# A graph network's front phase: node products as half-row matmuls, taken in pairs

## The chip, the cores and the metric

One Trainium2 core runs the whole program. The metric is device time in microseconds (us), the median of three runs. Five engines work side by side: PE (TensorE; its weight loads are listed as PEld), DVE (VectorE), ACT (ScalarE), POOL (GpSimd) and SP (SyncE, which here only issues DMAs). They meet through semaphores.

## The reference, cut to what matters

Two layers of a graph network over 6250 nodes and 100000 edges. The front phase, which the change touches, computes the part of layer 0 that joins each edge with its node:

```python
s1 = jnp.einsum('ea,eb,abc->ec', xs, es, W1) * (1.0 / np.sqrt(MUL0_N * MUL0_E))
s2 = jnp.einsum('eai,ebi,abc->ec', xv, ev, W2) * (1.0 / (np.sqrt(3.0) * np.sqrt(MUL1_N * MUL1_E)))
out_s = (s1 + s2) * inv_sqrt2
v1 = jnp.einsum('ea,ebi,abc->eci', xs, ev, W3) * (1.0 / np.sqrt(MUL0_N * MUL1_E))
v2 = jnp.einsum('eai,eb,abc->eci', xv, es, W4) * (1.0 / np.sqrt(MUL1_N * MUL0_E))
out_v = (v1 + v2) * inv_sqrt2
...
agg = jax.ops.segment_sum(messages, row, num_segments=N_NODES)
```

Here `xs` are 64 scalars of a node and `xv` 32 vectors of three components; an edge has 8 scalars and 8 vectors (32 numbers).

## The kernel before

The kernel first multiplies nodes with the weights, not edges: for each block of 128 nodes a table `g` of 32 rows of 160 numbers a node is made (rows stand for the 32 edge numbers). The table goes to memory (`products`) and comes back, four nodes together, into a ring in SBUF (`quad_ring`). An edge's message is then a product of its own 32 numbers, placed by DVE into `front_work` where its node stands, with that ring.

**Tiles, pairs, chunks.** The 784 tiles have 128 edges each. Two tiles are a pair, two pairs a batch, eight pairs (k = 0 to 7) a chunk of 16 tiles; there are 49 chunks, and 49 blocks of nodes. The loops are unrolled in Python (`unrolled`), so each engine's order is the order in which the code calls the stages.

**PE, in one pair k of chunk i:** in every even pair `spread_ids` (L517, one product of one row, bf16) for a batch two ahead; `expand` (L544 and L549): seven f32 products of 160 columns, which the trace shows as 14 matmuls; in every odd pair `expand` begins with `load_words`, a register load of PE (L476); last `produce`: `unit(i + 3, k)` for k below 6, and `rank` (L506, L507) in pair 6.

**A unit** is one sixth of a block's table. Units 0 to 3 are a product of 128 rows with 512 columns (L492), units 4 and 5 two of 256 columns (L495, L496), all f32; the trace shows each product as two matmuls. The operands `x_alone` hold 64 or 32 rows of node features and zeros in all others, so that a full-height product picks the wanted part of the weights `w_first` (wa) and `w_second` (wb). The units fill two PSUM banks in turn; unit n waits for `units_taken` of n-2.

**ACT** copies in program order: `copy_pair` (L642, L644: messages out of PSUM, which frees one of three banks for `expand`), in odd pairs `spread_features` (L633, three copies) for the batch four ahead, in pairs 3 and 7 the load of a ring unit (L623), and then `take_unit` (L598, L601 to L605) for the same k. After unit 5 it stores the table (L609).

**DVE**, batch by batch: `build` (L836 to L849: with a register load of its own, L842; needs the batch's ids, its features, and that the batch three before has been expanded); after the build of a chunk's first batch `settle_places` (L815 to L826), which waits for the `rank` that PE does in pair 6 of the chunk before; after that of the second batch `tally` (L796 to L804). PE's `spread_ids` for batch n waits until the batches up to n-2 are built, `expand` of batch n until n is built.

**POOL** scatters each tile's messages (L451). **SP** loads ids, features and, once a chunk, the node features of a block (L398 to L401).

## Time and profile before

| | |
|---|---|
| median of 3 runs | 3041.04 us (3039.52 to 3052.91) |
| time of the profiled execution | 3042.78 us, of it 3041.0 us span |
| front phase: first to last matmul of L549 | 51 to 1325 us |
| PE busy in the span | 85% |
| granted TensorE clock, mean of the span | 0.928 |

A row of a timeline reads: start, duration, engine, line, operation, count, and in brackets how long the engine was idle before it and who ended that. Matmuls overlap: two L549 that begin at 848.39 and last 0.43 are two of 0.30 that begin 0.14 apart. So PE's time is read from start to start. The ends are modelled, and some waits are put down to "remote" or "issue" where no releaser is shown.

### The profile page before, as it was taken

How to read it: one execution, taken by the hardware profiler on the slowest of the kernel's cores; microseconds unless marked ns; L12 is line 12 of the kernel's file. 1: busy time of each engine (PE TensorE's matmuls, PEld its weight loads, DVE VectorE, ACT ScalarE, POOL GpSimd, SP SyncE). 2: the span in 40 equal slices, each digit the busy share in tenths (PEclk: the TensorE clock that was granted, in tenths of full speed). 3: DMA queues.
4: the chain of work that ended last, by engine and by line, in shares of the span. 5: the costliest groups of instructions: out<-in, count | busy, mean ns of one | idle time of the engine just before them, and what ended most of it. 6: DMA issues, size and time to landing. Idle time of an engine off the chain costs nothing. (4 is left out here: it accounts for less than half of the span.)

```text
span 3041.0 us, 51486 instructions
## 1 busy us (share of the span) xinstructions
PE 2570.8 (85%) x15408; PEld 2273.6 (75%) x15408; DVE 1878.6 (62%) x5408; ACT 1082.7 (36%) x2570; POOL 1584.4 (52%) x1677
## 2 busy tenths in 40 slices
PE   6989988989999999879999578787788777777787
PEld 4777777777777777769999478777777777777777
DVE  6666666666666676648878455555555555554555
ACT  4555555555555555512222122212222222121211
POOL 3656565565656656631010356655566556555553
PEclk9999999999999999989999698988988889888888
DMA  7888888888878888747888422222222222222221
GB/s 277 288 289 295 300 299 300 294 288 275 274 259 274 276 280 264 233 185 265 285 290 288 128 67 69 64 67 79 63 68 68 73 67 68 66 63 79 63 66 49
DMA packets 417284, 558.62 MB, mean 184 GB/s; under 512 B 73425, under 2 KB 354880, under 8 KB 404549
## 3 DMA queue, kind: packets, MB, share of 16 engines
q10 hardware_dynamic: 217680, 262.22, 25.7%
q1 hardware_dynamic: 120694, 153.35, 15.7%
q0 software_dynamic: 78640, 139.64, 15.4%
q8 instruction: 145, 2.38, 0.3%
q14 instruction: 125, 1.02, 0.1%
HBM read 326.92 MB, written 228.11 MB: 183 GB/s over the span
## 5 line engine op out<-in xcount | busy, mean ns | idle before, releaser
L1551 POOL DMA_INDIRECT f_y<-y_table,b_rec x782 | 767.9, 982 | 548.0 <-DVE f_msg L1634 310.3
L451 POOL DMA_INDIRECT placed<-message,slots_now x784 | 770.0, 982 | 536.0 <-ACT message L644 319.7
L544 PEld LDWEIGHTS g_bank<-quad_ring,front_work 128*128 128x128 f32 x4704 | 671.5, 193 | 187.4 <-issue 184.5
L544 PE MATMUL g_bank<-quad_ring,front_work 128*128 x4704 | 748.7, 309 | 72.7 <-issue 55.6
L1760 PE MATMUL e_bank<-f_msg,f_hot 128*126 128x160 f32 x1564 | 356.7, 333 | 212.8 <-DVE f_msg L1634 191.4
L846 DVE SCALAR_TENSOR_TENSOR front_work<-g_bank,quarter_node,front_work 128x512 f32<-128x512 f32 x588 | 404.7, 744 | 153.1 <-issue 101.3
L1760 PEld LDWEIGHTS e_bank<-f_msg,f_hot 128*126 128x126 f32 x1564 | 273.4, 209 | 240.0 <-DVE f_msg L1634 214.8
L1755 PE MATMUL e_bank<-f_msg,f_hot 128*126 128x160 f32 x1564 | 383.1, 329 | 25.3 <-DVE f_msg L1634 13.0
L1844 ACT COPY block_sums<-e_bank 126x320 f32<-126x320 f32 x196 | 83.4, 425 | 810.6 <-PE e_bank L1755 387.7
L633 ACT COPY front_work<-front_work 32x512 f32<-32x512 f32 x588 | 362.4, 616 | 13.2 <-issue 3.6
L1744 PE MATMUL e_bank<-fc,b_hidden 100*128 100x192 f32 x1564 | 342.4, 341 | 10.5 <-issue 10.5
L1620 DVE TENSOR_TENSOR e_bank<-e_bank,own 128x6 f32<-128x6 f32 x195 | 33.4, 171 | 499.8 <-remote 322.3
L644 ACT COPY message<-g_bank 128x320 f32<-128x320 f32 x392 | 168.3, 432 | 459.7 <-PE g_bank L549 269.4
L1755 PEld LDWEIGHTS e_bank<-f_msg,f_hot 128*126 128x126 f32 x1564 | 293.7, 212 | 30.4 <-issue 23.0
L1744 PEld LDWEIGHTS e_bank<-fc,b_hidden 100*128 100x128 f32 x1564 | 286.8, 203 | 22.5 <-issue 15.1
L1606 DVE SCALAR_TENSOR_TENSOR f_hot<-count_row,b_column,b_rec 128x168 f32<-128x168 f32 x782 | 270.9, 387 | 0.6 <-issue 0.6
L1219 PE MATMUL z_bank<-big,work 128*128 128x161 f32 x1764 | 254.7, 302 | 10.7 <-DVE work L1134 10.5
L1219 PEld LDWEIGHTS z_bank<-big,work 128*128 128x128 f32 x1764 | 245.5, 191 | 11.2 <-issue 10.7
L1634 DVE TENSOR_TENSOR f_msg<-e_bank,f_y 128x192 f32<-128x192 f32 x782 | 238.3, 345 | 0.0
L492 PE MATMUL g_bank<-w_first,x_alone 128*128 128x512 f32 x392 | 203.2, 603 | 14.7 <-DVE w_second L682 13.4
L1838 ACT ACTIVATE b_hidden<-e_bank 100x512 f32<-100x512 f32 x196 | 117.0, 597 | 225.3 <-PE e_bank L1735 101.1
L1631 DVE TENSOR_TENSOR f_msg<-e_bank,f_y 128x256 f32<-128x256 f32 x391 | 162.6, 416 | 54.7 <-issue 21.2
(252 smaller groups left out, 3199.4 us busy)
## 6 DMA issues: line engine op xcount, KB each, us to landing
products<-g ACTq DMA_DIRECT2D x49, 2560.0 KB
quad_ring<-products ACTq DMA_DIRECT2D x98, 1280.0 KB
big<-placed SPq DMA_DIRECT2D x48, 1458.0 KB, 7.1
b_lengths<-length_parts SPq DMA_DIRECT2D x294, 60.0 KB
placed<-zeros SPq DMA_DIRECT2D x24, 648.0 KB
front_work<-in_e_t SPq DMA_DIRECT2D x196, 64.0 KB
placed<-message,slots_now POOLq DMA_INDIRECT x784
f_y<-y_table,b_rec POOLq DMA_INDIRECT x782
```

The costliest lines, as they stand in the source:

```text
L451: pool.indirect_dma_start(v.placed[:, :], bass.IndirectOffsetOnAxis(slots_now[tile // SET % SLOT_SETS][:, tile % SET:tile % SET + 1], 0), ...
L492: last = pe.matmul(into[:], xs[j][:], wa[:], start=True, stop=True)
L544: pe.matmul(bank_now[:, n * D:n * D + D], spread[batch % SPREADS][:, j, q * P:q * P + P], ring[:, bass.ds(slot + j, 1), :].rearrange("p a ...
L633: last = act.copy(features[h][32 * n:32 * n + 32, :, :], features[h][0:32, :, :])
L846: dve.scalar_tensor_tensor(spread[batch % SPREADS][:, j, :], p_node[h % 2][:], v.quarter_node[:, j:j + 1], flat, ALU.is_equal, ALU.mult)
L1219: last = pe.matmul(p_agg[k % 2], hot[k % 2][:, j, :], placed_rows[k][:, j, 0:MW], start=(j == 0), stop=(j == ROWS - 1))
L1551: pool.indirect_dma_start(f_y[:, at, :], None, v.y_table[:, :], bass.IndirectOffsetOnAxis(b_rec[d % LOAD_RING][:, b % LOADED, 2 * c + n, 0 ...
L1606: dve.scalar_tensor_tensor(f_hot[:, r, :, :], v.count_row[:, 0:SUB].unsqueeze(1).broadcast_to([P, 4, SUB]), b_column[b % COLUMNS][:, j:j + 1],
L1634: last = dve.tensor_tensor(f_msg[:, r + n, :, S:D].rearrange("p g (i c) -> p g i c", i=3), w[:, n, 128:192].rearrange("p (g c) -> p g c", ...
L1744: last = pe.matmul(p_rad[pair % 3][:, 192 * n:192 * n + 192], b_hidden[b % HIDDEN_RING][:, 2 * c + n, :], v.fc2[:], start=True, stop=True)
L1755: return pe.matmul(p_acc[b % 2][0:3 * SUB, D:MSG], f_hot[:, r, 1:4, :].rearrange("p s n -> p (s n)"), f_msg[:, r, 1, :], start=(c == 0 and ...
L1760: return pe.matmul(p_acc[b % 2][0:3 * SUB, 0:D], f_hot[:, r, 0:3, :].rearrange("p s n -> p (s n)"), f_msg[:, r, 0, :], start=False, stop=F ...
```

## The change

The zero-padded operands go. A block's features come in two tiles, `x_parts`: the first has the 64 scalars in rows 0 to 63, vector component 0 in rows 64 to 95 and zeros to 127; the second has component 2 in rows 0 to 31, zeros to 95, component 1 in rows 96 to 127. Each product now uses the upper 64 or the lower 64 rows alone; a new weight tile `w_upper` (wc) has the vector weights in its first 32 rows and zeros below. The units alternate: 0, 2, 4 upper, 1, 3, 5 lower. Two units stand together behind pair 1, 3 and 5, and ACT takes two behind its pair 0, 2 and 4. The number of products and of columns is as before. SP issues two loads of features a block in place of four. At the start ACT issues two more weight loads, and DVE scales two more weight pieces and clears less.

```diff
-        wa, wb = sb("w_first", [P, 512]), sb("w_second", [P, 256])
-        alone = [[sb(f"x_alone{k}{m}", [P, P]) for m in range(4)] for k in range(2)]
+        wa, wb, wc = sb("w_first", [P, 512]), sb("w_second", [P, 256]), sb("w_upper", [S, 768])
+        parts = [[sb(f"x_parts{k}{m}", [P, P]) for m in range(2)] for k in range(2)]
...
+                act.dma_start(wc[0:V, 0:512], t["w2"]).then_inc(weights_in, 16)
+                act.dma_start(wc[0:V, 512:768], t["w4"]).then_inc(weights_in, 16)
...
-                    for m in range(4):
-                        dve.memset(alone[k][m][:], 0.0)
+                    dve.memset(parts[k][0][96:P, :], 0.0)
+                dve.memset(wc[V:S, :], 0.0)
...
-                    one, two, three, four = alone[b % 2]
-                    sp.dma_start(one[0:64, :], t["x_t"][0:64, at]).then_inc(x_in[b % 2], 16)
-                    sp.dma_start(two[64:96, :], t["x_t"][64:96, at]).then_inc(x_in[b % 2], 16)
-                    sp.dma_start(three[96:128, :], t["x_t"][96:128, at]).then_inc(x_in[b % 2], 16)
-                    sp.dma_start(four[64:96, :], t["x_t"][128:160, at]).then_inc(x_in[b % 2], 16)
+                    sp.dma_start(parts[b % 2][0][0:96, :], t["x_t"][0:96, at]).then_inc(x_in[b % 2], 16)
+                    sp.dma_start(parts[b % 2][1][:], t["x_rest_t"][:, at]).then_inc(x_in[b % 2], 16)
...
-                    if j < 4:
-                        last = pe.matmul(into[:], xs[j][:], wa[:], start=True, stop=True)
+                    upper, lower = slice(0, S), slice(S, P)
+                    if j == 0:
+                        last = pe.matmul(into[:], first[upper, :], wa[upper, :], start=True, stop=True)
+                    elif j == 1:
+                        last = pe.matmul(into[:], first[lower, :], wa[lower, :], start=True, stop=True)
+                    elif j == 2:
+                        last = pe.matmul(into[:], rest[upper, :], wc[:, 0:512], start=True, stop=True)
+                    elif j == 3:
+                        last = pe.matmul(into[:], rest[lower, :], wa[lower, :], start=True, stop=True)
+                    elif j == 4:
+                        pe.matmul(into[:, 0:256], first[upper, :], wb[upper, :], start=True, stop=True)
+                        last = pe.matmul(into[:, 256:512], rest[upper, :], wc[:, 512:768], start=True, stop=True)
                     else:
-                        m = 2 * (j - 4)
-                        pe.matmul(into[:, 0:256], xs[m][:], wb[:], start=True, stop=True)
-                        last = pe.matmul(into[:, 256:512], xs[m + 1][:], wb[:], start=True, stop=True)
+                        pe.matmul(into[:, 0:256], first[lower, :], wb[lower, :], start=True, stop=True)
+                        last = pe.matmul(into[:, 256:512], rest[lower, :], wb[lower, :], start=True, stop=True)
...
-                    if k < PARTS6:
+                    if k % 2 and k < PARTS6:
+                        unit(i + LEAD, k - 1)
                         unit(i + LEAD, k)
...
-                    if k < PARTS6:
+                    if k % 2 == 0 and k < PARTS6:
                         take_unit(i + LEAD, k)
+                        take_unit(i + LEAD, k + 1)
```

On PE, behind pair 4 of a chunk, stands before (L549 ends pair 4, L495 and L496 are unit 4, L476 the register load ahead of pair 5):

```order
L549 MATMUL g_bank<-quad_ring,front_work 128x160
L495 MATMUL g_bank<-w_second,x_alone 128x256
L496 MATMUL g_bank<-w_second,x_alone 128x256
L476 TENSOR_LOAD places
L544 REGISTER_ALU
L544 ISA
L544 MATMUL g_bank<-quad_ring,front_work 128x160
```

and now, where L553 and L558 are the lines of the same expansion and L475 that of the register load:

```order
L558 MATMUL g_bank<-quad_ring,front_work 128x160
L475 TENSOR_LOAD places
L553 REGISTER_ALU
L553 ISA
L553 MATMUL g_bank<-quad_ring,front_work 128x160
```

The register load of pair 5 follows pair 4 with no unit between them.

On PE, behind pair 5, stands before (L495, L496: unit 5; L517: the ids product ahead of pair 6):

```order
L549 ISA
L549 REGISTER_ALU
L549 MATMUL g_bank<-quad_ring,front_work 128x160
L495 MATMUL g_bank<-w_second,x_alone 128x256
L496 MATMUL g_bank<-w_second,x_alone 128x256
L517 MATMUL g_bank<-id_rows,ones 128x512
L544 REGISTER_ALU
```

and now:

```order
L558 ISA
L558 REGISTER_ALU
L558 MATMUL g_bank<-quad_ring,front_work 128x160
L501 MATMUL g_bank<-w_second,x_parts 128x256
L502 MATMUL g_bank<-w_upper,x_parts 128x256
L504 MATMUL g_bank<-w_second,x_parts 128x256
L505 MATMUL g_bank<-w_second,x_parts 128x256
L526 MATMUL g_bank<-id_rows,ones 128x512
L553 REGISTER_ALU
```

Units 4 (L501, L502) and 5 (L504, L505) now both stand there; units 0 and 1, 2 and 3 stand so behind pairs 1 and 3.

On ACT, from pair 2 to pair 4, stands before (L598 is the take of units 2 and 3):

```order
L644 COPY message<-g_bank 128x2x160
L598 COPY g<-g_bank 128x8x64
L644 COPY message<-g_bank 128x2x160
L633 COPY front_work<-front_work 32x512 x3
L623 DMA quad_ring<-products 128x16x160
L598 COPY g<-g_bank 128x8x64
L642 COPY message<-local 128x4
L644 COPY message<-g_bank 128x2x160
```

and now, where L609 is the take, L655 the message copy and L644 the copy of features:

```order
L655 COPY message<-g_bank 128x2x160
L609 COPY g<-g_bank 128x8x64 x2
L655 COPY message<-g_bank 128x2x160
L644 COPY front_work<-front_work 32x512 x3
L634 DMA quad_ring<-products 128x16x160
L653 COPY message<-local 128x4
L655 COPY message<-g_bank 128x2x160
```

The take of unit 3 has moved ahead of the message copy and the feature copies of pair 3.

## Rows read from the trace of the kernel before

**Rows 1.** Busy time by stretch; then PEclk, DMA share, GB/s. The last is without products.

```profile
800.00:1000.00 200.00, 183.19 (x1049) 145.78 (x1048) 133.96 (x294) 115.03 (x266) 119.69 (x124) 0.99 0.84 276
1277.00:1303.00 26.00, 22.14 (x120) 19.31 (x119) 14.47 (x30) 13.50 (x28) 16.00 (x17) 0.87 0.37 113
```

**Rows 2.** Line L549: count, duration min/median/max in ns, first and last start.

```profile
L549 PE MATMUL g_bank<-quad_ring,front_work x784: 296/299/474, 51.0 to 1324.7; 128*128 x196
```

**Rows 3.** Waits from 76 to 1250 us (45 chunks): total, times, longest.

```profile
DVE held L815 <- PE g_bank L507: 131.5, 31, 9.0
...
DVE held L815 <- remote: 65.3, 11, 7.7
...
DVE slots_now L836 <- ACT message L644: 31.0, 19, 2.6
...
PE g_bank L517 <- DVE front_work L849: 25.9, 31, 2.1
...
PEld g_bank L495 <- ACT g L598: 15.2, 18, 1.8
```

**Rows 4.** Timeline of PE, one chunk, from rank to rank.

```profile
830.69 0.39 PE L507 MATMUL g_bank<-held,ones 128*128 128x49 f32 x2
...
837.13 1.89 PE L544 MATMUL g_bank<-quad_ring,front_work 128*128 x12 [0.81 <-issue]
...
845.17 1.02 PE L492 MATMUL g_bank<-w_first,x_alone 128*128 128x512 f32 x2
846.12 0.38 PE L517 MATMUL g_bank<-id_rows,ones 1*128 1x512 bf16 x1
...
848.66 0.59 PE L495 MATMUL g_bank<-w_second,x_alone 128*128 128x256 f32 x2
...
851.43 0.43 PE L549 MATMUL g_bank<-quad_ring,front_work 128*128 x2
852.55 0.70 PE L495 MATMUL g_bank<-w_second,x_alone 128*128 128x256 f32 x2 [0.68 <-ACT g L598]
853.09 0.59 PE L496 MATMUL g_bank<-w_second,x_alone 128*128 128x256 f32 x2
853.61 0.39 PE L517 MATMUL g_bank<-id_rows,ones 1*128 1x512 bf16 x1
...
856.09 0.39 PE L507 MATMUL g_bank<-held,ones 128*128 128x49 f32 x2
```

**Rows 5.** Timeline of DVE in the same chunk.

```profile
831.11 0.21 DVE L815 TENSOR_TENSOR held<-held,r_count 128x49 f32<-128x49 f32 x1 [3.03 <-PE g_bank L507]
...
845.18 0.60 DVE L849 SCALAR_TENSOR_TENSOR front_work<-g_bank,quarter_node,front_work 128x128 f32 x2
```

**Rows 6.** Timeline of ACT in the same chunk, pair 3.

```profile
849.57 0.43 ACT L644 COPY message<-g_bank 128x320 f32<-128x320 f32 x1 [2.56 <-PE g_bank L549]
...
850.02 1.87 ACT L633 COPY front_work<-front_work 32x512 f32<-32x512 f32 x3
851.91 0.58 ACT L598 COPY g<-g_bank 128x512 f32<-128x512 f32 x1
```

**Rows 7.** Timeline of PE in a chunk without products: pairs 1, 4 and 5.

```profile
1253.79 1.89 PE L544 MATMUL g_bank<-quad_ring,front_work 128*128 x12 [1.44 <-issue]
...
1266.37 0.43 PE L549 MATMUL g_bank<-quad_ring,front_work 128*128 x2
1267.30 1.89 PE L544 MATMUL g_bank<-quad_ring,front_work 128*128 x12 [0.50 <-issue]
```

**Rows 8.** Timeline of PE behind the loop: products of 128 and of 32 rows in turn.

```profile
1327.77 0.74 PE L573 MATMUL g_bank<-wu_bot,wm_t 128*33 128x160 f32 x2
1328.44 0.74 PE L574 MATMUL g_bank<-wu_bot,wm_t 32*33 32x160 f32 x2
```

**Rows 9.** Timelines of DVE and of PE at the start of the program.

```profile
11.80 0.86 DVE L682 TENSOR_SCALAR w_first<-w_first 64x512 f32<-64x512 f32 x2
...
13.36 3.61 PE L492 MATMUL g_bank<-w_first,x_alone 128*128 128x512 f32 x4 [13.36 <-DVE w_second L682]
```

More of the change, by code:

```diff
@@ L597, in take_unit @@
                     if j < 4:
-                        last = act.copy(into[:, 8 * j:8 * j + 8, 0:S], full[:].rearrange("p (b c) -> p b c", c=S))
+                        m = (0, 1, 3, 2)[j]
+                        last = act.copy(into[:, 8 * m:8 * m + 8, 0:S], full[:].rearrange("p (b c) -> p b c", c=S))
                     elif j == 4:
@@ L601, in take_unit @@
                             act.copy(into[:, 8 + 8 * c:16 + 8 * c, S + 32 * c:S + 32 * c + 32], eight[:, 0, :, :])
-                        last = act.copy(into[:, 0:8, S:S + 32], eight[:, 1, :, :])
+                        last = act.copy(into[:, 0:8, S + 64:S + 96], eight[:, 1, :, :])
                     else:
-                        act.copy(into[:, 0:8, S + 32:S + 64], eight[:, 0, :, :])
-                        last = act.copy(into[:, 0:8, S + 64:S + 96], eight[:, 1, :, :])
+                        act.copy(into[:, 0:8, S:S + 32], eight[:, 0, :, :])
+                        last = act.copy(into[:, 0:8, S + 32:S + 64], eight[:, 1, :, :])
                     last.then_inc(units_taken, 1)
@@ L2052 @@
         "x_t": parts_first(np.ascontiguousarray(x.T)),
+        "x_rest_t": np.concatenate([x.T[S + 2::3], np.zeros((S, NODE_ROWS), np.float32), x.T[S + 1::3]]),
         "src_rows": src.reshape(TILES, P), "dst_rows": dst.reshape(TILES, P),
```

11 lines of the change are left out of this document (6 added, 5 removed).

## The prediction

> **What bounds the kernel now.** First the busy time by stretch: from 800 to 1000 us PE is busy 183 of 200 us, DMA 0.84, and PE looks like the bound [rows 1]. But in the chunk from 1277 to 1303, when no table is made any more, the DMA share is 0.37 and a chunk still takes 26 us [rows 1]. The whole loop runs from 51 to 1325 us, 49 chunks of 26.0 us [rows 2]. So neither DMA nor the sum of PE's work alone sets the pace; something goes round in a circle.
>
> The waits name it. DVE stands before L815 for 131.5 and 65.3 us in 42 of 45 chunks: it waits for PE's rank, 4.4 us a chunk. PE in turn waits before the ids product L517 for DVE's build, 31 times, 25.9 us [rows 3]. The timelines of one chunk give the circle its lengths. PE's rank (L507) stands at 830.69, DVE begins to settle places at 831.11 [rows 4, 5]; with two builds and the tally it is done at 845.18 + 0.60 = 845.78 [rows 5]. PE issues L517 of pair 4 at 846.12, and the next rank at 856.09 [rows 4]. That is 25.4 us: 15.4 us in which DVE's leg runs, and 10.0 us of PE alone, pairs 4, 5 and 6 with **units 4 and 5**. Beside DVE's leg PE does pairs 7, 0, 1, 2, 3 with **units 0 to 3**, and in this chunk it ends them at the same moment: L492 of unit 3 starts at 845.17 and L517 follows without a wait [rows 4].
>
> So the six units do not count alike. A saving on units 4 and 5 shortens every chunk. One on units 0 to 3 counts only where PE and not DVE comes last, at most 45 - 31 = 14 chunks of 45; elsewhere PE waits longer, 25.9 / 31 = 0.84 us now.
>
> **Prices of a unit.** From L492 to the next L517 are 0.95 us, from L496 (256 columns) to L517 0.52 us [rows 4]. The difference, 0.43 us, is 256 columns of f32; so a unit takes 0.86 us, and 0.09 us is left for the change from a product of 128 rows to one of 1 row. Unit 5 also waits: pair 5 has its last matmuls from 851.43, two 0.14 us apart, so PE is free at 851.70, and unit 5 starts at 852.55, released by ACT's take of unit 3 (L598 at 851.91). That take stood behind the message copy and three feature copies of pair 3 [rows 4, 6]. Over the loop it is 15.2 us in 18 chunks [rows 3], 0.34 us a chunk.
>
> **The change, part by part.** All sums are per chunk; 45 chunks make products in the steady loop.
>
> *Half-row products.* Each product keeps its columns, so alone it costs what it costs now. A gain comes only if a lower product runs beside an upper one. No row of before has two such products. The bounds are no overlap (0.86 us a unit as now) and full overlap (two units in 0.86 us). I take a value between, because each f32 product is two matmuls, x2, in a row [rows 4]: if PE keeps the written order, the first lower one can start only when the last upper one starts. Of four equal pieces two run together: 0.43 us saved on units 0/1 and on 2/3; on 4/5, which are eight pieces, one of eight, 0.21 us.
>
> *Change of height.* The half-row pair is entered from 128-row products, and left to L517, which is a change now too. So one change a pair is new, 0.09 us by the L517 row; behind the loop, where rows alternate between 128 and 32 at the low clock, two matmuls take 0.67 us from start to start [rows 8], 0.14 us more than two of 0.27. Bounds 0 and 0.14; I take 0.09. The Trainium skill, TensorEngine Tiling (Array Packing), Key Properties, says that a change of tiling mode drains the TensorE, which speaks against six short visits a chunk; the 0.09 us of this trace is what such a drain costs here, so this leaves the sum as it is.
>
> *The register load loses its cover.* Pairs 1, 3 and 5 begin with L476, a register load. Before, a unit of the even pair lay between the expansion and it and kept PE's array busy meanwhile; now it follows the expansion directly. The chunks at the end without products show that case: 0.50 us of "issue" before pair 5, and 1.44 us before pair 1, where now it is 0.81 us in the chunk shown [rows 7, 4]. The 0.50 us lies in PE's own leg, in every chunk. Bounds 0 and 1.44.
>
> *ACT takes two at once.* The takes of units 2 and 3 now stand ahead of pair 3's message and feature copies (1.87 us), so the wait for unit 3's take should go: -0.34 us. In return pair 3's message copy is late by up to the unit pair and two takes, 1.3 + 2 x 0.58 = 2.5 us. What hangs on it is DVE's L836, which waits for that copy (31.0 us in all [rows 3]) ahead of the build before L815. DVE's 4.4 us before L815 cover it; without that cover it would cost the 2.5 us in each chunk. PE has three banks for pairs and isn't held.
>
> *SP and the start.* Two loads a block instead of four; SP isn't in the circle. At the start the first product waits for the scaling of the weights at 13.36 us, of which one piece takes 0.43 us [rows 9]; two more pieces are at most 0.9 us, once. I count 0.
>
> The sum in PE's own leg: units 4 and 5 now 0.86 + 0.86 + 0.34 = 2.06 us; after, 1.72 - 0.21 + 0.09 + 0.50 = 2.10 us. So +0.04. Beside DVE: -2 x 0.43 + 2 x 0.09 + (1.44 - 0.81) = -0.05 us, in 14 chunks of 45, hence -0.02. Together +0.02 us x 45 = +1 us: what the overlap and the vanished wait bring, the uncovered register load takes back. The profiled execution took 3042.8 us, 1.7 above the median; from the median I forecast **3041 us**, no change that a measurement tells.
>
> **The rivals.**
> 1. *Both halves fully side by side.* Units 4 and 5 take 0.86 us instead of 1.51: -0.65; beside DVE another 2 x 0.43 in 14 of 45 chunks: -0.27. 0.92 x 45 = 41 us: **3000 us**. Against it: PE issues two matmuls per product one after the other [rows 4]. The Trainium skill, TensorEngine Tiling (Array Packing), Theoretical Speedup, gives up to 2x for a contraction of 64 rows or fewer, which is this case; its TensorE: Matmul & The Clock Gate, Part 3, says that matmuls keep their order, which is my case. No row here decides.
> 2. *The register load costs nothing* because the sequencer is far enough ahead: -0.50 x 45 = -22 us, **3019 us**. For it: behind pair 4 PE has waited for DVE in most chunks and the sequencer with it. Against it: that holds in the chunk of 1266.37 too, and there the 0.50 stands [rows 7].
> 3. *Slower: no overlap at all.* Then +0.21 in PE's leg, and +0.86 - 0.05 = +0.81 beside DVE, which counts in 14 chunks of 45 (elsewhere the 0.84 us of waiting covers it): +0.25. 0.46 x 45 = 21 us: **3062 us**. It decides from about a quarter of the overlap that I assume missing on every pair.
> 4. *Slower: the register load of pair 5 waits for an empty array*, as that of pair 1 does, 1.44 us instead of 0.50: +0.94 x 45 = 42 us, **3083 us**. It ends beyond what can be told from no change once the gap passes 0.50 + 15 / 45 = 0.83 us.
> 5. *ACT's takes come as late as before*: PE's signals reach ACT late in pair 3 (2.56 us of wait at 849.57 [rows 6]), and then unit 4 waits where unit 5 did. +0.34 x 45 = 15 us: **3056 us**.
> The clock is 0.99 in the loop and 0.87 where products are gone and PE has gaps [rows 1]; PE keeps most of its work here, so I give a fall of the clock no case of its own.
>
> **How the numbers follow.** Chances: forecast 0.36 (3033 to 3049, all within 0.5%, 15 us, which is about what a measurement of this kernel can tell from no change); rival 1 0.20 and rival 2 0.14, both faster by more; rival 3 0.10, rival 4 0.10, rival 5 0.10, slower. So faster 0.34, same 0.36, slower 0.30. The range runs from rival 1 to rival 3 with a few us at each end, 2996 to 3065; rival 4 and the tails are left out. The forecast's own range is 3033 to 3049, from 0.2 us a chunk each way.
>
> **What would show it.** In the timeline of PE: the starts of the four matmuls of units 0 and 1. If the third starts at the second's start, the order is kept and they overlap as I assume; 0.43 us behind it, nothing overlaps; at the first's, both halves run side by side. Their distance from L549 before and L517 after tells the price of the change of height. Before pair 5 a gap of 0.5 us. The row "PEld L495 <- ACT" should be gone. The wait of DVE before L815 should stay near 4.4 us, with L517 waiting for DVE in more chunks than 31. Wrong would be the forecast if the loop's length changed by more than 0.3 us a chunk; a start that moves by more than 1 us, or a change outside 51 to 1325 us, would be outside my reckoning.

## The result and the profile after

The changed kernel takes 3083.5 us (median, 3070.2 to 3093.6) where the kernel before takes 3047.0 us in the same comparison: a ratio of 1.0098, with a 95% interval of 1.0062 to 1.0135. So it is about 1% slower. The forecast was no change, 3041 us, and a range of 2996 to 3065 us. Its profiled execution took 3078.9 us, 3077.1 us of it span.

First the stages, by the rows of the expansion's last matmul, to be held against [rows 2] (L558 is now the line of L549):

```profile
L558 PE MATMUL g_bank<-quad_ring,front_work x784: 296/299/474, 55.7 to 1344.5; 128*128 x196
```

The loop starts 4.7 us later (55.7 against 51.0), lasts 1288.8 us instead of 1273.7 (+15.1), and what lies behind it takes 1732.6 us instead of 1716.3 (+16.3), although its instructions are the same. The third part turns out below to be a difference between executions and not the change's. So the profiles give the change some 20 us (0.65%); the ratio's 1.0% has them inside its interval, near its lower end.

The timeline of PE answers [rows 4]. A row is start, duration, engine, line, operation, count, and in brackets how long the engine was idle and who ended that:

```profile
830.07 0.43 PE L558 MATMUL g_bank<-quad_ring,front_work 128*128 x2
830.43 0.69 PE L493 MATMUL g_bank<-w_first,x_parts 64*128 64x512 f32 x1
830.44 0.69 PE L495 MATMUL g_bank<-w_first,x_parts 64*128 64x512 f32 x1
830.97 0.59 PE L493 MATMUL g_bank<-w_first,x_parts 64*128 64x512 f32 x1
830.97 0.59 PE L495 MATMUL g_bank<-w_first,x_parts 64*128 64x512 f32 x1
831.49 0.38 PE L526 MATMUL g_bank<-id_rows,ones 1*128 1x512 bf16 x1
...
846.38 0.39 PE L516 MATMUL g_bank<-held,ones 128*128 128x49 f32 x2
...
850.71 0.43 PE L558 MATMUL g_bank<-quad_ring,front_work 128*128 x2
852.98 2.16 PE L553 MATMUL g_bank<-quad_ring,front_work 128*128 x12 [1.83 <-issue]
```

Two things are to be seen. Unit 0 (L493, upper rows) and unit 1 (L495, lower rows) start within 0.01 us of each other, and so do their second matmuls: they run fully side by side. And behind pair 0 (850.71) PE now stands idle for 1.83 us before pair 1 begins; it was 0.81 us in [rows 4].

The timelines of DVE and of ACT in the same chunk:

```profile
842.70 0.17 DVE L848 COPY slots_now<-slot 128x8 int32<-128x8 int32 x1 [2.83 <-ACT message L655]
...
849.47 0.21 DVE L827 TENSOR_TENSOR held<-held,r_count 128x49 f32<-128x49 f32 x1 [3.45 <-remote]
```

```profile
841.20 0.59 ACT L609 COPY g<-g_bank 128x512 f32<-128x512 f32 x1 [4.14 <-remote]
...
841.68 0.59 ACT L609 COPY g<-g_bank 128x512 f32<-128x512 f32 x1
842.16 0.45 ACT L655 COPY message<-g_bank 128x320 f32<-128x320 f32 x1
```

PE had ended units 2 and 3 (L497, L499) by 837; ACT takes them at 841.20, the message copy of pair 3 stands behind that at 842.16, and DVE's L848 waits for it until 842.70. PE's rank (L516) stands at 846.38, but DVE settles the places (L827) only at 849.47, 3 us after it: the signal is late. In [rows 5] it took 0.42 us (830.69 to 831.11).

The waits from 76 to 1250 us, to be held against [rows 3] (total, times, longest):

```profile
ACT g L609 <- remote: 140.4, 27, 8.4
...
DVE held L827 <- PE g_bank L516: 111.6, 24, 6.1
...
DVE held L827 <- remote: 69.2, 18, 7.0
DVE slots_now L848 <- ACT message L655: 64.3, 22, 5.1
...
PE g_bank L526 <- DVE front_work L861: 24.4, 20, 3.4
PE g_bank L553 <- ACT message L655: 22.6, 13, 3.0
```

PE's weight load waits for ACT's take 1.3 us in all now instead of 15.2. DVE's wait for a message copy has doubled (31.0 to 64.3 us), and PE waits for DVE's build 20 times instead of 31. Of PE's own waits the one with no releaser before the first products of a pair has grown most ("issue"; the gap behind pair 0 is one of them). Its row before, and then changed:

```profile
PE g_bank L544 <- issue: 45.7, 51, 3.0
```

```profile
PE g_bank L553 <- issue: 100.1, 100, 3.5
```

**The circle, cut in four.** With R the end of a rank on PE, chunks 4 to 46, the means of: R to DVE's start on `held` (the signal); from there to the end of the build that PE's third ids product of the chunk waits for (DVE); from that to the ids product (PE behind); from the ids product to the next R (PE's leg).

| | signal | DVE | PE behind | PE's leg | period | loop | ratio to before |
|---|---|---|---|---|---|---|---|
| before | 0.88 | 14.78 | 0.29 | 10.20 | 26.15 | 1273.7 | |
| changed | 1.34 | 14.70 | 0.82 | 9.73 | 26.59 | 1288.8 | 1.0098 |

So by these two profiles the change made PE's own leg 0.47 us shorter, and lost 0.46 us in the lateness of one signal and 0.53 us because PE is later than DVE. A second profile of the kernel before (e8) makes the three 0.34, 0.33 and 0.40 us: the signs hold, the sizes are good to some 0.15 us. The ids product of pair 4 was issued over 0.45 us behind DVE's build in 6 of 43 chunks before and in 18 in the changed kernel.

### The profile page after: what moved, and what is told of

It is laid out like the page before. It is cut to its first block and busy times, and to the rows that moved or that the text cites. A ratio compares the mean times of both kernels' runs of the same rounds, so it can differ in the third digit from the quotient of the medians.

```text
span 3077.1 us, 51387 instructions
## 1 busy us (share of the span) xinstructions
PE 2525.3 (82%) x15408; PEld 2237.5 (73%) x15408; DVE 1880.2 (61%) x5405; ACT 1079.6 (35%) x2570; POOL 1591.5 (52%) x1677
## 3 DMA queue, kind: packets, MB, share of 16 engines
q0 software_dynamic: 78640, 139.64, 15.1%
q14 instruction: 124, 1.02, 0.1%
## 5 line engine op out<-in xcount | busy, mean ns | idle before, releaser
L553 PE MATMUL g_bank<-quad_ring,front_work 128*128 x4704 | 772.8, 315 | 143.9 <-issue 106.5
L553 PEld LDWEIGHTS g_bank<-quad_ring,front_work 128*128 128x128 f32 x4704 | 680.8, 197 | 219.3 <-issue 218.3
L1767 PE MATMUL e_bank<-f_msg,f_hot 128*126 128x160 f32 x1564 | 380.6, 327 | 15.1 <-issue 8.1
L644 ACT COPY front_work<-front_work 32x512 f32<-32x512 f32 x588 | 362.4, 616 | 11.4 <-DMA front_work<-in_e_t 1.3
L1756 PE MATMUL e_bank<-fc,b_hidden 100*128 100x192 f32 x1564 | 351.0, 346 | 14.1 <-issue 13.5
L655 ACT COPY message<-g_bank 128x320 f32<-128x320 f32 x392 | 165.9, 429 | 282.2 <-remote 200.8
L1109 POOL DMA_DIRECT2D length_parts<-work x48 | 25.7, 542 | 324.3 <-ACT work L1326 322.4
```

The source lines that it names most:

```text
L553: pe.matmul(bank_now[:, n * D:n * D + D], spread[batch % SPREADS][:, j, q * P:q * P + P], ring[:, bass.ds(slot + j, 1), :].rearrange("p a ...
L644: last = act.copy(features[h][32 * n:32 * n + 32, :, :], features[h][0:32, :, :])
L1756: last = pe.matmul(p_rad[pair % 3][:, 192 * n:192 * n + 192], b_hidden[b % HIDDEN_RING][:, 2 * c + n, :], v.fc2[:], start=True, stop=True)
L1767: return pe.matmul(p_acc[b % 2][0:3 * SUB, D:MSG], f_hot[:, r, 1:4, :].rearrange("p s n -> p (s n)"), f_msg[:, r, 1, :], start=(c == 0 and ...
```

## Experiments

All of them ran in five rounds beside the kernel before, each round on another chip. Three chips are alike (before: 3058, 3061, 3028 us; e1 to e12); on the two others, **chips B** (e13 to e16 on one, e17 and e18 on the other), the kernel before takes 2639 us. Loops are from the first to the last L549 or L558, as above.

### Which part of the change costs: e1, e2

e1 keeps the half-row products but puts one unit and one take behind each pair, as before:

```diff
-                    if k % 2 and k < PARTS6:
-                        unit(i + LEAD, k - 1)
+                    if k < PARTS6:
                         unit(i + LEAD, k)
...
-                    if k % 2 == 0 and k < PARTS6:
+                    if k < PARTS6:
                         take_unit(i + LEAD, k)
-                        take_unit(i + LEAD, k + 1)
```

> The changed kernel with its half-row products and two loads a block, but one unit behind each of the pairs 0 to 5 and one take behind each, as before. No upper and lower product stand next to each other, so nothing can overlap. Theory A (the loss comes from where the units and the takes stand: uncovered register load, message copies held up): within 0.3% of the kernel before, 3041 to 3050 us, a start later by 4 to 5 us included. Theory B (the half-row products or the extra weight pieces cost the time): as slow as the changed kernel, about 1.0% over before, 3075 us or more. The granted clock should stand at about 0.928 by theory A.

e2 is the opposite: the kernel before with the changed kernel's places for units and takes (the diff above, reversed).

> The kernel before with its full-height, zero-padded products and four loads, but two units behind pairs 1, 3 and 5 and two takes behind ACT's pairs 0, 2 and 4, as changed. Theory A: slower than the changed kernel by the overlap that is missing (two units 1.7 us instead of about 1.0, 0.65 us on 4/5 and part of the rest): 1.5 to 2.5% over before, 3087 to 3117 us. Theory B: within 0.3% of before, since full-height products are cheap in any order: 3038 to 3050 us. The gap ahead of pair 1's products should be 2.5 us and ahead of pair 5's 0.5 to 0.6 us by theory A.

e1: 3064.1 us, ratio 1.0030 (1.0005 to 1.0055). e2: 3082.0 us, 1.0082 (1.0051 to 1.0113), as slow as the changed kernel within the intervals. So the places cost most of the 1%, theory A, though e2 lost about half or less of what A had expected (1.5 to 2.5%); the half-row products do not take any of it back that can be told. The timelines of PE, first of e1 and then of e2, give the price of a unit:

```profile
830.92 0.43 PE L558 MATMUL g_bank<-quad_ring,front_work 128*128 x2
831.29 1.12 PE L499 MATMUL g_bank<-w_first,x_parts 64*128 64x512 f32 x2
832.34 0.39 PE L526 MATMUL g_bank<-id_rows,ones 1*128 1x512 bf16 x1
...
834.39 0.43 PE L558 MATMUL g_bank<-quad_ring,front_work 128*128 x2
834.75 0.70 PE L501 MATMUL g_bank<-w_second,x_parts 64*128 64x256 f32 x2
835.29 0.59 PE L502 MATMUL g_bank<-w_upper,x_parts 64*128 64x256 f32 x2
835.81 1.90 PE L553 MATMUL g_bank<-quad_ring,front_work 128*128 x12
```

```profile
838.55 0.43 PE L549 MATMUL g_bank<-quad_ring,front_work 128*128 x2
838.83 1.88 PE L492 MATMUL g_bank<-w_first,x_alone 128*128 128x512 f32 x4
840.64 0.38 PE L517 MATMUL g_bank<-id_rows,ones 1*128 1x512 bf16 x1
```

A lone half-row unit makes it 1.42 us from L558 to the ids product and 1.42 us to the next expansion. Over the loop the shortest intervals from one pair's last matmul to the next's are 3.47 us with a half-row unit and ids product between (3.28 with a full-height one) and 3.15 us with a half-row unit alone (2.76). So a visit to half height costs 0.19 us ahead of an ids product and 0.39 us ahead of an expansion. Two full-height units and the ids product make 4.13 us, the half-row pair 3.48: it still saves 0.65 us.

The Trainium skill (TensorEngine Tiling (Array Packing), Key Properties) says that a change of tiling mode drains the TensorE. The trace agrees in that a visit costs time, the 0.19 and 0.39 us above, where I had put 0.09; that it is a drain no row shows. The Trainium skill (TensorE: Matmul & The Clock Gate, Part 3) says that matmuls keep their order in start and end. Here the lower product's first matmul starts at 830.44, ahead of the upper product's second at 830.97, so the order of the products in the program isn't the order of the starts, and the measurement decides.

### ACT's takes, or PE's register load: e3, e4

e3 moves the changed kernel's takes one pair later on ACT (`if k % 2 and k < PARTS6: take_unit(i + LEAD, k - 1); take_unit(i + LEAD, k)`), so that no message copy stands behind a wait for a unit pair.

> The changed kernel with one thing moved: ACT takes both units behind its pairs 1, 3 and 5 instead of 0, 2 and 4, so that no message copy of pairs 1, 3 and 5 stands behind a wait for a unit pair. Theory A1 (the held-up message copies are the loss; expansion waits for them 25.5 us, DVE's slots 64 us against 31 before): the loss of 36 us turns into a gain, 3010 to 3035 us, and the row of PE waiting for ACT's message copy falls back to under 10 us. Theory A2 (the uncovered register load is the loss, 1.5 us more before pair 1 and 0.6 before pair 5): within 0.4% of the changed kernel, 3070 to 3090 us.

e4 moves the changed kernel's unit pairs one pair earlier on PE:

```diff
-                    if k % 2 and k < PARTS6:
-                        unit(i + LEAD, k - 1)
+                    if k % 2 == 0 and k < PARTS6:
                         unit(i + LEAD, k)
+                        unit(i + LEAD, k + 1)
```

> The changed kernel with its unit pairs behind PE's pairs 0, 2 and 4 instead of 1, 3 and 5; ACT's takes stay behind its pairs 0, 2 and 4. So each register load of pairs 1, 3 and 5 stands behind a unit pair again, and the takes wait less long. Theory A1 or A2, either: the overlap is left as the only effect, 20 to 45 us under before, 3000 to 3025 us; the gap ahead of pair 1 falls from 2.6 to under 1 us. If A2 alone holds, it is faster than the kernel with late takes by over 20 us; if A1 alone holds, both are within 10 us of each other. Theory B: no better than the changed kernel, 3070 us or more.

e3: 3086.7 us, 1.0100 (1.0065 to 1.0134), no better than the changed kernel, as theory A2 said. The message copy of pair 1 is early again (9.59 us behind R as before, 12.48 in the changed kernel), yet the time stays: the copies held up by the takes are not the loss. e4: 3044.9 us, 0.9970 (0.9946 to 0.9993), 1.3% under the changed kernel by one place, but 13 us under before and not the 20 to 45 that either theory had expected. Its loop:

```profile
L558 PE MATMUL g_bank<-quad_ring,front_work x784: 296/299/474, 56.0 to 1314.0; 128*128 x196
```

The mean intervals from pair to pair say where. Over the shortest such interval (1.90 us without a unit between, 3.16 with the pair) the interval from pair 0 to 1 holds 2.57 us of waiting in the changed kernel (mean 4.47) and 1.38 in e4 (4.54); the other seven differ by 0.1 us together. Before it was 1.11 us (3.87 over 2.76). Between these kernels the gap behind pair 0 is the place of the difference.

### The register load itself: e5, e6

Both make PE's register load (L475) at the start of the even pair instead of the odd one, e5 on the changed kernel, e6 on e4:

```diff
-                    if pair % 2 == 1:
+                    if pair % 2 == 0:
                         load_words(batch + 1)
```

> The changed kernel with one thing moved: PE's register load of a batch's places stands at the start of the even pair ahead, behind the ids product and, for pairs 2, 4 and 6, behind a unit pair, instead of at the start of the odd pair with nothing between it and the expansion. Units and takes stay where the change put them. Theory A (the uncovered register load costs the time): pairs 1 and 5 follow pairs 0 and 4 after 1.9 us instead of 4.3 and 2.6 (medians), the load in front of pair 0 gets a gap of its own of 0.5 to 1.5 us, and the kernel gains 15 to 35 us on the changed one, 3045 to 3065 us on a chip where before takes 3050. Theory T (the takes and the message copies behind them cost it): within 0.3% of the changed kernel, 3075 to 3090 us.

> Unit pairs behind PE's pairs 0, 2 and 4 and the register load at the start of the even pair, so the load stands behind nothing but the ids product. Theory A: the load now has less cover than behind a unit pair, in all of pairs 0, 2, 4 and 6, while pairs 1, 3 and 5 lose nothing; 0 to 15 us slower than the kernel with the units behind the even pairs, 3045 to 3060 us. If the bubble ahead of pair 1 (1.1 us over the shortest) came from the load's own length and not from its cover, it goes to pair 0 and the time stays, 3040 to 3048 us.

e5: 3083.2 us, 1.0078 (1.0059 to 1.0098), the same as the changed kernel within its interval, where theory A had expected 15 to 35 us less. The interval from pair 0 to 1 is down to 2.04 us (mean), but the one from 7 to 0 has grown from 2.62 to 3.75 and that from 3 to 4 from 4.16 to 5.62: the gap has moved. e6: 3083.7 us, 1.0072 (1.0049 to 1.0095), 1.0% slower than e4 (each against before on its own chip), more than I expected, by nothing but the load's place: behind a unit pair it is covered, behind an ids product it isn't.

The load's durations explain why pair 1 is special. It is not counted as busy time, but its rows stand in the trace (ns min/median/max; the changed kernel, PE's load and DVE's, 76 to 1250 us):

```profile
L475 PEldq TENSOR_LOAD <-places x177: 327/1002/3788, 77.8 to 1246.8; - x177
```

```profile
L854 DVEq TENSOR_LOAD <-places x177: 528/548/2260, 79.4 to 1246.6; - x177
```

PE's load ahead of pair 1 takes 3.50 us (median), ahead of pairs 3 and 7 0.33, ahead of pair 5 1.08. All 45 that lie beside the packets with which a block's table is stored take 3.40 us or more; the 132 others have a median of 0.47 and at most 1.52. The kernel before has the same 3.45 us, but unit 0 stood ahead of it and kept PE's array busy. DVE's load beside the store takes 1.77 us, elsewhere 0.54.

### The overlap without the bad place: e7, and a second look at before: e8

e7 has before's full-height products at e4's places.

> The kernel before with its full-height products and four loads, two units behind pairs 0, 2 and 4, takes behind ACT's pairs 0, 2 and 4. Against the kernel with half-row units at the same places it tells what the overlap brings: two full-height units take 1.72 us, the half-row pair 1.05. If the 0.67 us counts for units 4 and 5 alone, it is 45 x 0.67 = 30 us slower than that kernel in the loop, less 5 us that its start is earlier: 25 us slower, 3065 to 3075 us. If little of it counts, because the price of the changes of height and ACT's takes set the pace, it is 0 to 10 us slower: 3040 to 3055 us.

> The kernel before, unchanged, for a second profile: how far its stages vary from one execution to the next. The part behind the loop took 1716 us in the first profile of before and 1729 to 1737 us in four with half-row products, with the same instructions. If that is a difference of executions, this profile lies anywhere from 1712 to 1737 us; if the changed kernel makes it, it lies within 3 us of 1716. The ratio to before should be 1.000.

e7: 3050.0 us, 0.9958 (0.9943 to 0.9972). It has e4's gain without its overlap. In the loop e4 is 4.6 us shorter (1258.0 against 1262.6), and its start is 3.7 us later. The overlap is worth nothing that can be told. The clock may hide a part of it (below, the table of runs).

e8: ratio 1.0003 (0.9983 to 1.0023). Its loop took 1277.0 us and the part behind it 3055.1 - 1328.0 = 1727.1 us, 10.8 more than in the first profile. Over all profiles on the three like chips that part lies between 1699 and 1748 us (e7: 3063.0 - 1314.9), with no order by kernel. So the 16.3 us there are not the change's. Three profiles of loops like before's (before, e8, e9) lie within 4 us; single profiles can still mislead, since e3's execution was the fastest of its six (3068.6 us, median 3086.7) and e7's the slowest of its seven (3064.7, median 3050.0).

### The store in small pieces: e9 to e12

If the 20480-byte packets of the store hold up the register loads, small ones should not:

```diff
-                        act.dma_start(v.products[b * P:b * P + P, :], into[:].rearrange("p b d -> p (b d)")).then_inc(g_out[b % 2], 16)
+                        for half in range(2):
+                            act.dma_start(v.products[b * P:b * P + P, :].rearrange("p (x y e) -> p x y e", x=4, y=2)[:, :, half, :],
+                                          into[:].rearrange("p (x y c) d -> p x y (c d)", x=4, y=2)[:, :, half, :]).then_inc(g_out[b % 2], 16)
```

The two waits for `g_out` count twice as far. It is put on before (e9), changed (e10), e7 (e11) and e4 (e12).

> The kernel before with one thing changed: the store of a block's table goes out as two DMAs of 2560-byte pieces instead of one of 20480-byte pieces. In the traces so far PE's register load takes 3.45 us (median of 50) where it lies beside packets of 20480 bytes and 0.37 us (130) elsewhere, DVE's 1.77 us (47) and 0.55 us (133). Theory S (the big packets hold up the register loads): both fall below 1.2 us in every place, the gap ahead of pair 1 goes, DVE's leg of the circle is 1.2 us shorter, 1 to 2% faster than before, 3000 to 3030 us. Theory P (the place in the chunk and not the packets makes the loads long, for example DVE's own work beside them): they stay at 3.4 and 1.8 us and the time within 0.4% of before.

> The changed kernel with the table stored in 2560-byte pieces. Theory S: the register load of pair 1, which no unit covers here, falls from 3.5 to about 1 us, so the changed kernel's loss against the kernel before with the same store shrinks from 1.0% to the later start, 0.2%, or turns to a gain of up to 0.5%: 2995 to 3035 us. Theory P: 3075 to 3090 us, 1.0% over the kernel before with the same store.

> Full-height products, two units behind pairs 0, 2 and 4, and the table stored in 2560-byte pieces. Theory S: the gains add up only as far as DVE's leg lets them, 1.0 to 2.5% under before, 2985 to 3025 us. Theory P: as with the large pieces, 0.4% under before, 3040 to 3055 us.

> Half-row products, two units behind pairs 0, 2 and 4, and the table stored in 2560-byte pieces. It tells whether the overlap is worth anything once the register loads are short: by theory S, if PE's own leg then sets the pace, 0.67 us a chunk and up to 30 us less than with full-height products at the same places, less the 4 us of the later start; if DVE's leg sets it, within 5 us of them. 2975 to 3025 us.

Ratios: e9 1.0027 (1.0007 to 1.0047), e10 1.0106 (1.0066 to 1.0145), e11 0.9963 (0.9935 to 0.9991), e12 0.9965 (0.9942 to 0.9989). The pieces are small now (50176 of 2560 bytes, none of 20480), and the loads as long as ever, here in e10:

```profile
L475 PEldq TENSOR_LOAD <-places x178: 327/1005/4185, 75.9 to 1244.7; - x178
```

48 of them take over 1.3 us, with a median of 3.6. Theory S falls: it isn't the packets' size. That the loads are long while a table is stored stands; whether the store or something else at that time does it isn't shown. The four also repeat the comparison: places 1.4% (e10 against e12), overlap nothing (e11, e12). And e10 tells something of the cause on a like chip: the rank's signal is early there (0.32 us), yet the loop is 12 us longer than e9's, with PE 1.63 us behind DVE against 0.43 and a mean of 5.22 us from pair 0 to 1 against 3.72. So there PE's lateness is enough for the loss, without a late signal of the rank.

### The load taken out of the store's time: e13 to e18, on chips B

```diff
-                    if pair % 2 == 1:
+                    if pair % 2 == 1 and (k != 1 or i == 0):
                         load_words(batch + 1)
+                    if k == 7:
+                        load_words(batch + 2)
```

e13 is the changed kernel so, e14 the kernel before. In e15 (on e7) and e16 (on e4) DVE's load of a chunk's second batch is made with the first batch's as well.

> The changed kernel; PE's register load of pair 1 (3.5 us, beside the store of a table) is made in pair 7 of the chunk before, behind that pair's own load (0.33 us), before the store is issued. Theory L (this load, uncovered since the units moved, is the loss): the interval from pair 0 to pair 1 falls from 4.3 to 1.9 to 2.5 us, the order's 1.3 us of loss on PE's way to the ids product of the chunk's third batch is gone, and the kernel is 15 to 35 us faster than the changed one, 0 to 0.5% faster than the kernel before. Theory M (ACT's paired takes and the message copies behind them are the loss, the load only fills time): within 0.3% of the changed kernel, 0.8 to 1.1% over before.

> The kernel before with the same move of PE's register load of pair 1 into pair 7. Its load is partly covered by unit 0, so less is to be had: the interval from pair 0 to pair 1 falls from 3.8 to 2.8 us. DVE's leg of 15.7 us sets the pace there, so theory L expects 0 to 0.4% under before (3 to 12 us); if the circle were PE's in most chunks, 1.0 us x 45 = 45 us.

> Full-height products, two units behind pairs 0, 2 and 4; PE's register load of pair 1 made in pair 7, and DVE's register load of a chunk's second batch (1.77 us, on DVE's leg between settling the places and the build) made with the first batch's. DVE's leg is then 1.2 us shorter in each of 45 chunks: 20 to 50 us less than the same kernel without the moves, 1.0 to 2.0% under before. If DVE's load is as long at its new place, or another wait takes its part, 0.3 to 0.6% under before.

> As the last, with the half-row products that run side by side. If PE's leg sets the pace after DVE's is shorter, the overlap now counts: 0.46 us a chunk (the shortest interval from pair 4 to 5 is 3.17 against 3.63 us), 20 us less in the loop, 5 us more at the start, so 0.5% faster than full height. If other waits set it, within 0.2% of full height.

Ratios: e13 0.9968 (0.9954 to 0.9981), e14 1.0039 (1.0025 to 1.0053), e15 1.0401 (1.0385 to 1.0416), e16 0.9966 (0.9952 to 0.9980). By itself e13 looks like theory L. But this chip is not like the first three, so the changed kernel was run as it is beside the moved load, on another chip that turned out to be of the same kind:

> The changed kernel as it is, on the same chip as the next run. If this chip is like the first ones (before near 3045 us), 1.0% over before, as measured. If it is like the last one (before near 2640 us): theory L (the long register load behind pair 0 is the loss) expects 0.5 to 1.0% over before there as well; if that chip alone turned the sign, it is 0.3% under before already.

> The changed kernel with PE's register load of pair 1 made in pair 7 of the chunk before. Theory L: at least 0.6% faster than the changed kernel in the same call, whichever chip it is; on a chip like the first ones 0 to 0.4% over or under before, with the interval from pair 0 to pair 1 at 1.9 us. Theory M (paired takes and held-up message copies): within 0.3% of the changed kernel.

e17, the changed kernel: 2633.6 us, 0.9977 (0.9965 to 0.9989). e18: 2631.9 us, 0.9971 (0.9960 to 0.9981). **On chips B the change makes the kernel 0.23% faster**, and the load's place adds nothing that can be told, although the mean interval from pair 0 to 1 falls from 3.77 to 1.90 us. There PE then waits for DVE instead; e18's timeline of PE behind units 0 and 1, a wait of 0.79 us:

```profile
857.93 0.59 PE L493 MATMUL g_bank<-w_first,x_parts 64*128 64x512 f32 x1
857.94 0.59 PE L495 MATMUL g_bank<-w_first,x_parts 64*128 64x512 f32 x1
859.32 0.37 PE L526 MATMUL g_bank<-id_rows,ones 1*128 1x512 bf16 x1 [0.79 <-DVE front_work L863]
```

Theory L, which asked for 0.6%, falls for chips B. The same load is as long there: ahead of pair 1 it takes 3.61 us (median) in e17. e14 missed too: 0 to 0.4% under before were expected of the moved load, and it is 0.39% over; why, no run tells. With the load moved in both kernels, e14 and e18, the change is worth 0.7% (1.0039 against 0.9971, each against before on its own chip), the loop 34 us shorter (1199.2 against 1165.6).

What is different on chips B is seen at once in e17's waits of DVE and ACT; none of its rows has "remote":

```profile
DVE held L827 <- PE g_bank L516: 186.3, 45, 8.6
...
ACT g L609 <- PE g_bank L495: 156.7, 39, 6.5
...
ACT g L609 <- PE g_bank L499: 61.9, 45, 1.5
PE g_bank L553 <- ACT message L655: 45.7, 31, 1.6
```

Counted over the message copies between 76 and 1250 us: a copy is late if it starts over 1 us behind both its pair's last matmul and ACT's previous operation. In the kernel before 92 of 360 are late, by 297 us together, up to 5.5 each; in the changed one 57 of 354, by 197 us. On chips B, in e14, e17 and e18, none of some 385. On the like chips the number of late copies does not order the kernels: e4 and e7, which are faster than before, have 119 and 110 of some 360. And most of the 400 us between the kinds of chip isn't in the loop: behind it e14 takes 1408 us and before 1716.

e15 is the one large loss, and it shows the cover again. DVE's part falls to 12.80 us as meant. But with the units one pair earlier and the load of two batches in pair 7, the second load now falls into the store's time, behind the rank:

```profile
849.20 0.39 PE L507 MATMUL g_bank<-held,ones 128*128 128x49 f32 x2
851.83 2.29 PE L546 MATMUL g_bank<-quad_ring,front_work 128*128 x12 [2.24 <-issue]
```

The interval from pair 6 to 7 is 5.78 us instead of 2.4. In e16 it is 4.55, and the intervals with units (0 to 1, 2 to 3, 4 to 5) are 0.46 us shorter each than e15's: 1.38 us x 45 = 62 us of the 123 us between their loops, the pair 6 interval 1.23 x 45 = 55 us. Here PE sets the pace (it is 4.98 and 2.53 us behind DVE), and here the overlap counts in full. The 55 us are not the overlap; in part they can be the clock, which is 0.95 in e15 and 0.98 in e16: behind the gap above the next two expansions begin with rows of 2.29 and 2.60 us, and behind the same gap in e16 with 1.89 and 1.90.

### The runs in one table

| | signal | DVE | PE behind | PE's leg | period | loop | ratio | clock |
|---|---|---|---|---|---|---|---|---|
| e8 before again | 1.01 | 14.78 | 0.42 | 10.07 | 26.28 | 1277.0 | 1.0003 | 0.98 |
| e1 half rows, single | 0.84 | 14.73 | 1.02 | 9.80 | 26.39 | 1281.8 | 1.0030 | 0.99 |
| e2 full height, pairs | 1.42 | 14.56 | 1.05 | 9.65 | 26.68 | 1298.8 | 1.0082 | 0.98 |
| e3 late takes | 0.98 | 14.77 | 0.52 | 10.12 | 26.39 | 1281.3 | 1.0100 | 0.97 |
| e4 half rows, even | 0.87 | 14.73 | 0.40 | 9.87 | 25.87 | 1258.0 | 0.9970 | 0.97 |
| e5 load early | 0.46 | 14.70 | 0.47 | 10.84 | 26.47 | 1291.9 | 1.0078 | 0.95 |
| e6 as e4, load early | 1.22 | 14.65 | 0.52 | 10.10 | 26.49 | 1295.9 | 1.0072 | 0.95 |
| e7 full height, even | 1.01 | 14.72 | 0.41 | 9.80 | 25.94 | 1262.6 | 0.9958 | 0.99 |
| e9 before, small store | 0.70 | 14.87 | 0.43 | 10.20 | 26.20 | 1273.5 | 1.0027 | 0.98 |
| e10 changed, small store | 0.32 | 14.86 | 1.63 | 9.56 | 26.38 | 1285.5 | 1.0106 | 0.95 |
| e11 as e7, small store | 0.29 | 14.76 | 0.63 | 9.81 | 25.49 | 1241.2 | 0.9963 | 1.00 |
| e12 as e4, small store | 0.87 | 14.69 | 0.56 | 9.46 | 25.58 | 1248.8 | 0.9965 | 0.98 |
| e13 changed, load moved (B) | 0.04 | 14.76 | 0.15 | 9.16 | 24.10 | 1164.5 | 0.9968 | 0.99 |
| e14 before, load moved (B) | 0.04 | 14.78 | 0.18 | 9.85 | 24.85 | 1199.2 | 1.0039 | 0.99 |
| e15 as e7, loads moved (B) | 0.04 | 12.80 | 4.98 | 8.91 | 26.73 | 1282.4 | 1.0401 | 0.95 |
| e16 as e4, loads moved (B) | 0.04 | 12.75 | 2.53 | 8.72 | 24.04 | 1159.3 | 0.9966 | 0.98 |
| e17 changed (B) | 0.04 | 14.65 | 0.24 | 9.15 | 24.08 | 1165.7 | 0.9977 | 0.99 |
| e18 changed, load moved (B) | 0.04 | 14.76 | 0.18 | 9.12 | 24.10 | 1165.6 | 0.9971 | 1.00 |

DVE's part is 14.6 to 14.9 us in all of them but e15 and e16, where its load was moved. What differs is the signal, how far PE is behind, and PE's leg.

The last column is the granted TensorE clock as a mean from 100 to 1150 us. Its records hold two levels alone, 1 and one half of it (2.4 and 1.2 GHz). The rows of the kernel before and of the changed one, from 100 to 1200 us (engines' busy times; the clock is the third number from the end):

```profile
100.00:1200.00 1100.00, 998.08 (x5723) 800.42 (x5722) 733.12 (x1638) 626.97 (x1431) 661.37 (x675) 0.99 0.86 285
```

```profile
100.00:1200.00 1100.00, 934.97 (x5621) 753.58 (x5619) 721.82 (x1612) 613.53 (x1404) 655.32 (x662) 0.97 0.85 282
```

By the records the changed kernel is at the lower level for 68 of these 1100 us, before for 24 and e8 for 34. PE is busy for 63 us less in it, and with more idle time on PE goes a lower clock. Of the half-row kernels on the like chips e3, e5, e6 and e10, which lose, stand at 0.95 to 0.97. It isn't the whole of the loss: e4 stands at 0.97 too, and its loop is 16 us shorter than before's; and e2 loses at 0.98. But no run holds the clock still, so what it costs the changed kernel, and what of the overlap it takes back in e4 (e7, without overlap, stands at 0.99), is open.

## Why the prediction was wrong

**The circle was right.** Rank, DVE's leg, ids product, PE's leg, rank: its four parts add up to the period in every run, and "a saving on units 4 and 5 shortens every chunk" holds where it can be seen best, on chips B with the same load moved in both kernels: PE's leg goes from 9.85 (e14) to 9.12 us (e18), the period from 24.85 to 24.10.

**The step that failed is "One on units 0 to 3 counts only where PE and not DVE comes last".** It was right for savings and was used for losses too. A loss beside DVE's leg makes PE the last one. PE behind went from 0.29 to 0.82 us as a mean of all chunks: +0.53 us x 45 = 24 us (18 by e8's 0.42), where I had put -0.02 x 45. Its number of chunks was misread too: the 31 waits before L517 are of all ids products, and only 19 of them stand ahead of pair 4's, the one in the circle (9 in the changed kernel), the others ahead of pair 2's.

**What made PE late, as far as the intervals tell, was the register load, mis-sized at pair 1.** I took 1.44 against 0.81 us, +0.63, from a chunk without products; in it no table is stored, and that hid the term. Measured, the waiting behind pair 0 went from 1.11 to 2.57 us, +1.46. The load behind pair 4 was sized well: the median interval is 2.57 over 1.90, 0.67 us, for my 0.50. Rival 4 gives the measured 3083 us by luck, with a mechanism that did not happen, a gap of over 0.83 us ahead of pair 5; its place was pair 1.

**The overlap: rival 1's mechanism, not its time.** That PE "keeps the written order" is refuted by the starts. The pair saves 0.65 us, its change of height paid, instead of my 0.43 less 0.09. But a lone visit costs 0.19 to 0.39 us, and 0.47 us off PE's leg in the changed kernel has a twin in e2, 0.55 us off, with no overlap at all. I take it that the ids product starts later there and what pair 4 waits for is ready; no run tests that.

**The take wait** went as said: PE's weight load waits 1.3 us for ACT in all, where it was 15.2. That the late message copy is covered by DVE's wait before the rank also held (e3).

**What I had no term for** is the signals' lateness. It stood in the rows: "remote" 65.3 us before L815 in [rows 3], and 2.56 us before a copy in [rows 6], which rival 5 used for ACT alone. The rank's signal came 0.46 us later on average in the changed kernel: 21 us (15 by e8's profile).

The signs that I had named went the other way too: DVE's wait before the rank fell from 4.4 to 4.0 us a chunk, and PE waited for DVE's build 20 times and not more than 31.

**The clock** I gave no case, because PE "keeps most of its work". In the loop it went from 0.99 to 0.97, and no term of the sum stands for that.

**The start** was put at most 0.9 us later and counted as 0; it moved by 4.7 us, which I had named as outside my reckoning. The scaling is 0.4 us of it. The rest arises in the three blocks made before the loop. Timelines of PE for one block, before and then changed:

```profile
34.07 5.28 PE L492 MATMUL g_bank<-w_first,x_alone 128*128 128x512 f32 x8
39.19 0.60 PE L495 MATMUL g_bank<-w_second,x_alone 128*128 128x256 f32 x2
```

```profile
36.91 1.22 PE L493 MATMUL g_bank<-w_first,x_parts 64*128 64x512 f32 x1
36.91 1.22 PE L495 MATMUL g_bank<-w_first,x_parts 64*128 64x512 f32 x1
...
39.73 1.22 PE L497 MATMUL g_bank<-w_upper,x_parts 64*128 64x512 f32 x1 [0.74 <-ACT g L609]
...
42.48 0.79 PE L501 MATMUL g_bank<-w_second,x_parts 64*128 64x256 f32 x1 [0.19 <-ACT g L609]
```

Both banks now fill at the same moment, so PE waits for both takes and ACT for both units. Units 0 to 3 take 5.57 us (36.91 to 42.48) instead of 5.12 (34.07 to 39.19), with PE idle between. And PE is on the lower clock: in the changed kernel every 512-column matmul of the three blocks takes 1.05 to 1.22 us, before most take 0.59 to 0.70, and only the first four and those at a granted clock of 0.5 (from 30.3 to 37.2 us) more. What the idle time and what the clock costs here, no run separates.

**What stays open.** Shown is that the places of the units cost the loss on the three like chips. How much of the 15 us of the loop is the load behind pair 0, how much the signals that come late there and how much the clock isn't shown; the load was moved away from the store on chips B alone. Why chips B have no late signals, and what makes a register load long while a table is stored, no run tells. The lowest ratio on the like chips is e7's, 0.42% under before, without half-row products; e4's, e11's and e12's cannot be told from it.

## What to carry to other kernels

Work that fills a gap ahead of a register load can be part of the circle even when it is not on the path: before moving it, ask what is then uncovered, and take the load's duration at that moment of the chunk and not from another stage. A loss beside the longer leg is not bound by the number of chunks in which it counts today. Two products that run side by side into two buffers also fill them together: here they paid where PE set the pace (e16 against e15) and not where DVE did (e4 against e7). And what makes an engine idler can lower its clock: look at the granted clock before and after.

## What was unexpected in the hardware

- f32 products on the upper and the lower 64 rows ran fully side by side: four matmuls start at 830.43, 830.44, 830.97 and 830.97.
- A lone visit to half height costs 0.19 us ahead of a one-row product and 0.39 us ahead of a full-height one (shortest intervals, e1 against before).
- A register load of PE takes 0.33, 1.08 or 3.50 us by its place in the chunk, DVE's 0.54 or 1.77; the long ones lie beside the store of a table, whether in 20480- or in 2560-byte packets.
- Of five chips two ran the kernel before in 2639 us instead of 3028 to 3061. The profiles taken there have no late signals (0 of some 385 copies, against 92 of 360 before), and the same change had the other sign on the one where it was run.
- With more idle time on PE the granted clock stood lower: 0.97 with 935 of 1100 us busy, 0.99 with 998.
